# Attention and mixture-of-experts block on one core: half of the first quad's score maxima taken inside the feature loop, and the last chunk's waves and features moved into the first quad

## The reference, cut to what matters

```python
x = _layernorm(x + attention(x))       # x: (2, 2048, 256), f32
x = _layernorm(x + moe_ffn(x))         # 8 experts, the top 2 per token

# attention, 16 heads of 16 dimensions
q, k, v = split(x @ Wq), split(x @ Wk), split(x @ Wv)
q_amp, k_amp = _amp_norm(q), _amp_norm(k)      # softplus, then divided by the root mean square over a head
q_phi = math.pi * jnp.tanh(split(x @ Wqp))
k_phi = math.pi * jnp.tanh(split(x @ Wkp))
scores_phase = (q_amp*cos(q_phi)) . (k_amp*cos(k_phi)) + (q_amp*sin(q_phi)) . (k_amp*sin(k_phi))
scores = (q . k + lam * scores_phase) / 4      # causal
out = softmax(scores) @ v @ Wo
```

## Time and profile before

| what | us |
|---|---|
| runs: median (lowest to highest of 3) | 1952.91 (1946.81 to 1959.45) |
| the profiled execution, its own time | 1948.98 |
| its span, first to last instruction | 1947.3 |
| PE busy, 89% of the span | 1737.1 |
| DVE busy, 65% | 1262.3 |
| ACT busy, 45% | 882.6 |
| POOL busy, 19% | 366.4 |
| mean granted TensorE clock, share of full speed | 0.941 |

### The profile page before, as it was taken

How to read it: one execution, slowest core, us unless ns; L and a number is a source line. 1 busy time by engine, 2 the same in 40 slices (tenths; PEclk the granted TensorE clock), 3 DMA queues, 4 the chain that set the end, 5 groups by cost and what they waited for, 6 DMA issues and landing times.

```text
span 1947.3 us, 28314 instructions
## 1 busy us (share of the span) xinstructions
PE 1737.1 (89%) x9130; PEld 920.4 (47%) x9131; DVE 1262.3 (65%) x2992; ACT 882.6 (45%) x1035; POOL 366.4 (19%) x478
## 2 busy tenths in 40 slices
PE   6998479999999999999999999977639999999965
PEld 3444234444444444444444444426525666666644
DVE  3677867777777777777777777516525555555536
ACT  2677524455555555555455554544311221221236
POOL 0111211111121111211211112103572111111111
PEclk9999768899999999999999999997759999999988
DMA  3366434011021020110201103016521111111144
GB/s 102 137 238 236 179 129 147 7 36 70 8 73 39 15 90 7 57 50 7 99 12 39 67 7 121 13 60 204 205 95 38 47 43 48 44 43 49 44 132 151
DMA packets 99497, 155.30 MB, mean 80 GB/s; under 512 B 10752, under 2 KB 60736, under 8 KB 99008
## 3 DMA queue, kind: packets, MB, share of 16 engines
q1 hardware_dynamic: 84928, 122.53, 18.9%
q0 software_dynamic: 14464, 31.40, 4.6%
HBM read 87.90 MB, written 65.35 MB: 79 GB/s over the span
## 4 chain that ended last, share of the span: by engine, by line
PE 70%; DVE 8%; ACT 7%; issue 6%; DMA 5%; POOL 2%; SPq 1%; another core or an unknown queue 0%; ACTq 0%; DVEq 0%; POOLq 0%
PE att_ps_s L884 22%; PE exp_ps_h L1564 13%; PE att_ps_o L903 12%; PE att_ps_m L862 10%; PE exp_ps_y L1582 6%; ACT att_probs L931 3%; DMA out_parts<-att_out_t 2%; PE pre_ps_q L311 2%; PE exp_ps_t L1572 2%; PE pre_ps_h L311 1%; DVE att_maxima L945 1%; DMA k_parts<-pre_waves 1%; PE exp_ps_x L1553 1%; POOL sorted_rows L1449 1%; DMA route_a_inv<-inv_rows 1%
## 5 line engine op out<-in xcount | busy, mean ns | idle before, releaser
L931 ACT ACTIVATE att_probs<-att_ps_s 128x1024 f32<-128x1024 f32 (+3 forms) x640 | 563.7, 895 | 484.4 <-PE att_ps_s L884 476.5
L884 PE MATMUL att_ps_s<-att_queries,att_keys 49*128 49x512 f32 (+3 forms) x2560 | 632.8, 561 | 20.9 <-ACT att_probs L931 11.4
L945 DVE TENSOR_REDUCE att_maxima<-att_ps_m 128x1 f32<-128x512 f32 x768 | 487.1, 684 | 153.6 <-PE att_ps_m L862 148.6
L862 PE MATMUL att_ps_m<-att_keys,att_queries 48*128 48x512 f32 (+3 forms) x1280 | 506.5, 605 | 24.1 <-DVE att_maxima L948 15.9
L862 PEld LDWEIGHTS att_ps_m<-att_keys,att_queries 48*128 48x128 f32 x1280 | 197.7, 193 | 315.8 <-DVE att_maxima L945 141.4
L884 PEld LDWEIGHTS att_ps_s<-att_queries,att_keys 49*128 49x128 f32 x2560 | 242.9, 191 | 127.3 <-ACT att_probs L931 85.4
L948 DVE CUSTOM_DVE_ANT_0 att_ps_m<-att_ps_m,att_future 128x128 f32<-128x128 f32 (+3 forms) x512 | 240.3, 514 | 73.4 <-PE att_ps_m L862 72.1
L903 PE MATMUL att_ps_o<-att_probs,att_values 128*32 128x512 f32 (+3 forms) x2560 | 269.3, 535 | 11.1 <-POOL att_probs L1034 11.1
L1564 PE MATMUL exp_ps_h<-keep_w,exp_rows_t 128*128 x568 | 257.4, 596 | 5.5 <-DVE exp_rows_t L1598 5.5
L1640 ACT ACTIVATE exp_hidden<-exp_product 128x512 f32<-128x512 f32 x71 | 44.8, 632 | 343.7 <-DVE exp_product L1623 343.7
L1034 POOL TENSOR_SCALAR_AFFINE_SELECT att_probs<-att_probs 128x512 f32<-128x512 f32 x128 | 81.1, 634 | 491.3 <-ACT att_probs L931 491.2
(11 more groups left out here) (179 smaller groups left out, 1458.6 us busy)
## 6 DMA issues: line engine op xcount, KB each, us to landing
att_queries<-q_parts SPq DMA_DIRECT2D x64, 192.0 KB
att_keys<-k_parts SPq DMA_DIRECT2D x64, 192.0 KB
exp_rows<-sorted_rows SPq DMA_DIRECT2D x71, 129.0 KB, 2.3
v_rows<-pre_v_sb SPq DMA_DIRECT2D x8, 1024.0 KB, 7.1
q_parts<-pre_waves SPq DMA_DIRECT2D x16, 512.0 KB, 4.2
k_parts<-pre_waves SPq DMA_DIRECT2D x16, 512.0 KB, 5.8
att_values<-v_rows SPq DMA_DIRECT2D x32, 256.0 KB
out_parts<-att_out_t POOLq DMA_DIRECT2D x32, 256.0 KB, 6.0
```

Of the source, the lines that this page charges most:

```text
L862: pe.matmul(take()[:, 0:width], queries[g % 2][half, c, r, P * q:P * q + P], keys[g % 2][half, k, r, 0:width], start=True, stop=True).then ...
L884: mm = pe.matmul(score_tile(unit, first, last)[:, e], keys[g % 2][half, k // TPC, r, P * (k % TPC):P * (k % TPC) + P].bitcast(F32), querie ...
L931: act.activation(probs[:, step % PROBS, DUO * r:DUO * r + DUO, first:last], score_tile(unit, first, last), ACT.Exp, scale=SCALE).then_inc( ...
L945: dve.tensor_reduce(to, buf[:, 0:width], AX.X, ALU.max).then_inc(s_mr, 1)
```

## The change

1. `Maxima` holds what the maxima need, and is made before `prepare`. In the passes of the feature loop that project chunks 4 to 7, PE puts two products of the maxima behind each half projection (`send_early`, eight times a pass), and DVE has eight `take_early` in its list, which take those two tiles each. Together these are the first 64 of quad 0's 160 tiles: chunks 0 and 1 whole, and a third of chunk 2. They use a ring of two banks: the products of a turn wait until the tiles of the turn before are read.
2. The banks of that ring come from `ps_n`: the norm sum of the queries now goes to `ps_q`, with two waits more (L519 waits for both copies of q, the projection of q for the logarithm of that sum).
3. The square of the amplitudes goes from POOL to ACT, as the second stage of its list, behind the first tanh and ahead of the norm's exponential.
4. On DVE the cosine features (`features`, f = 0) now stand ahead of `keep_qk` of the keys, where they stood behind it.
5. PE's list is unrolled.
6. Chunk 7's cosine and sine (ACT) and its features (DVE) are left out of `prepare`. ACT does them ahead of the exponentials of step 4 of quad 0, DVE at the values of step 3.
7. `Plan` begins with those 64 tiles done, and has the costs of item 6. The ones under the keys of the second buffer are written by SP instead of POOL, behind the last store of the features.

```diff
-            def square(i, p):
-                pool.wait_ge(s_amp, i + 1)
-                if since(i, 1):
-                    pool.wait_ge(s_norm, 2 * i)
-                pool.tensor_tensor(amp_sq[:, :], amp[:, p], amp[:, p], ALU.mult).then_inc(s_sq, 1)
-
-            pipelined(pool, NCH, [(square, 1)])
...
+    def send_early(self, pe):
+
+        for _ in range(DUO):
+            tile, self.sent = self.sent, self.sent + 1
+            if tile >= len(self.ring):
+                pe.wait_ge(self.s_mr, tile - len(self.ring) + 1)
+            self.send(pe, self.ring[tile % len(self.ring)], *self.early[tile])
+
+    def take_early(self, dve):
+
+        if self.taken == 0:
+            dve.wait_ge(self.s_const, 1)
+        for _ in range(DUO):
+            tile, self.taken = self.taken, self.taken + 1
+            self.take(dve, self.ring[tile % len(self.ring)], tile, *self.early[tile])
...
-            def project(weight, out, p):
+            def project(i, weight, out, p, ready):
 
                 for c in range(2):
                     for k in range(DK):
                         mm = pe.matmul(out[:, c], weights[:, weight, k, c * P:(c + 1) * P], x_t[:, p, k],
                                        start=(k == 0), stop=(k == DK - 1))
-                return mm
+                    if c == 1:
+                        mm.then_inc(ready, 1)
+                    if i in EARLY_CHUNKS:
+                        maxima.send_early(pe)
...
+            def square(i, p):
+                act.wait_ge(s_amp, i + 1)
+                if since(i, 1):
+                    act.wait_ge(s_norm, 2 * i)
+                act.activation(amp_sq[:, :], amp[:, p], ACT.Square).then_inc(s_sq, 1)
...
             pipelined(act, NCH, [
                 (lambda i, p: phases(i, p, Q), 1),
+                (square, 2),
                 (lambda i, p: norm_exp(i, p) if i < NCH - 1 else None, 3),
                 (soft_exp, 1),
...
             pipelined(dve, NCH, [
+                (take_early, 1),
                 (lambda i, p: keep_qk(i, p, Q), 1),
+                (take_early, 1),
                 (abs_phase, 2),
+                (take_early, 1),
                 (norm_amplitudes, 3),
+                (take_early, 1),
+                (lambda i, p: features(dve, i, p, 0) if i < NCH - 1 else None, 3),
+                (take_early, 1),
                 (lambda i, p: keep_qk(i, p, K), 1),
-                (lambda i, p: features(i, p, 0), 3),
+                (take_early, 1),
+                (take_early, 1),
+                (take_early, 1),
                 (keep_v, 1),
                 (amplitudes, 1),
                 (keep_x, 0),
-                (lambda i, p: features(i, p, 1), 3)])
+                (lambda i, p: features(dve, i, p, 1) if i < NCH - 1 else None, 3)])
...
             for step in range(QUADS * STEPS):
+                if step == LATE_STEP:
+                    features.last_waves(act)
...
                 elif event == "values":
                     keep_out(*what)
+                    if tuple(what) == (0, LATE_STEP - 1):
+                        features.last_features(dve)
```

More of the change, by code:

```diff
@@ L164, in absolute @@
     return dve.tensor_scalar(out.bitcast(U32), in_.bitcast(U32), 0x7FFFFFFF, None, ALU.bitwise_and)
-def prepare(nc, block, small, x, Wq, Wk, Wv, Wqp, Wkp, lambda_raw, q_parts, k_parts, v_rows, first_quad):
+BLOCKS = [TPC * (c + 1) for c in range(QC)]
+FIRST = [sum(BLOCKS[:c]) for c in range(QC)]
+STEPS = sum(BLOCKS)
+QUADS = B * NQ
+CHUNKS = QUADS * QC
+QUAD_LOADS = 16 * (2 * DUO + 1)
+MAX_TILES = [DUO * DUO * TPC * (c + 1) for c in range(QC)]
+SLOTS_PS = 3
+SLOTS_S = 2
+PROBS = 6
+BATCH = 2
+AHEAD = 3
@@ L172, in prepare @@
+def prepare(nc, block, small, x, Wq, Wk, Wv, Wqp, Wkp, lambda_raw, q_parts, k_parts, v_rows, first_quad, maxima):
     with ExitStack() as stack:
@@ L241, in prepare, with make_waves, features, last_waves @@
         rows_v = v_rows.rearrange("(c t p) w -> c p t w", p=P, t=TPC)
+        def make_waves(act, i, p):
+            act.wait_ge(s_absp, i + 1)
+            act.activation(waves[:, p, 0], waves[:, p, 0], ACT.Sin, bias=half_pi, scale=-PI_BELOW).then_inc(s_wave[0], 1)
+            act.wait_ge(s_tanh, 2 * i + 2)
+            if since(i, 2):
+                act.wait_ge(s_out[2][p], STORED * (i >> 1))
+            act.activation(waves[:, p, 1], phase[:, p], ACT.Sin, scale=PI_BELOW).then_inc(s_wave[1], 1)
+        def features(dve, i, p, f):
+            dve.wait_ge(s_an, i + 1)
+            dve.wait_ge(s_wave[f], i + 1)
+            for c in range(2):
+                dve.scalar_tensor_tensor(waves[:, p, f, c], normed[:, c], lam_scale[:, c:c + 1], waves[:, p, f, c],
+                                         ALU.mult, ALU.mult).then_inc(s_feat, 1)
+            dve.tensor_tensor(waves[:, p, f, 2:4], normed[:, 2:4], waves[:, p, f, 2:4], ALU.mult).then_inc(s_feat, 1)
+        def last_waves(act):
+            make_waves(act, NCH - 1, (NCH - 1) % 2)
+        def last_features(dve):
+            for f in range(2):
+                features(dve, NCH - 1, (NCH - 1) % 2, f)
         @block.sync
@@ L595, in __init__ @@
         self.kept_at, self.negated_at, self.placed_at = {-1: 0}, {}, {}
+        self.group = EARLY_GROUPS
+        self.turns = list(range(self.groups[EARLY_GROUPS][0]))
+        self.negated_at = {n: 0 for n in self.turns}
     def run(self, engine, ns, ready):
@@ L814, in attend, with put_ones @@
         vacated = {"max": s_mr, "turn_max": s_row}
-        CONSTS = 1
-        LOADS = 16 * (2 * DUO + 1)
+        def put_ones(eng, i):
+            eng.wait_ge(s_made, 1)
+            for e in range(DUO):
+                row = HALF * e + FEAT
+                eng.dma_start(keys[i][row:row + 1].rearrange("p c r t -> p (c r t)").bitcast(F32),
+                              ones[0:QC * DUO * CH // (P // 2)]).then_inc(s_one[i], 16)
         def chunk_row(g, c):
@@ L853, in take @@
                 return ps_m[buffer]
-            def max_tile(n, r, q, k, e):
-                g, c = divmod(n, QC)
-                if (r, q, e) == (0, 0, 0):
-                    pe.wait_ge(s_qkv[g % 2][c], LOADS * (g // 2 + 1))
-                width = CH if k < c else P * (q + 1)
-                half = slice(HALF * e, HALF * e + FEAT)
-                pe.matmul(take()[:, 0:width], queries[g % 2][half, c, r, P * q:P * q + P],
-                          keys[g % 2][half, k, r, 0:width], start=True, stop=True).then_inc(s_mt, 1)
             def turn_max(n):
@@ L913, in _ @@
                 elif event == "max":
-                    max_tile(*what)
+                    highest.send(pe, take(), *what)
                 elif event == "turn_max":
@@ L977, in invert @@
                 dve.reciprocal(inverse[:, n % 2], sums[:, n % 2]).then_inc(s_inv, 1)
-            tile = 0
+            tile = DUO * EARLY_GROUPS
             for event, *what in plan:
                 if event == "max":
-                    take_max(*what, tile, ps_m[slots.pop(0)[0]])
+                    highest.take(dve, ps_m[slots.pop(0)[0]], tile, *what)
                     tile += 1
-                    if tile == sum(MAX_TILES[m % QC] for m in range(what[0] + 1)):
-                        negate(what[0], tile)
                 elif event == "turn_max":
@@ L1002, in _ @@
             pool.memset(ones[:, :], 1.0).then_inc(s_made, 1)
[L1003 to L1016 removed]
+            put_ones(pool, 0)
+            made.make(pool)
             def place_max(n):
```

218 lines of the change are left out of this document (110 added, 108 removed).

## The result

The changed kernel takes 1982.46 us (median of 4 runs, 1976.50 to 1986.53) against 1952.75 us before (4 runs, 1946.81 to 1959.45): a ratio of 1.0143, with a 95% interval of 1.0114 to 1.0172. It is slower by 1.4%, within 1.5 us of the forecast. The profiled execution took 1986.53 us, and its span 1984.9.

What follows compares the result with a forecast made beforehand. A pass was taken to be bound by a chain of waits of nearly 24 us through the engines. Loop +49, last pass and drain +15.3, first quad -36.3: +28 us, 1981 us against 1952.91; range 1969 to 1993.

Steps and rivals of the forecast that it cites:

- Passes 2 and 3: Loop passes of chunks 2 and 3: square and cosine features join the chain, 28.3 us each, +8.8 us in all.
- The square: On ACT in each pass, ahead of the norm's exponential that DVE waits for: +1.9 us, no table load.
- The features ahead of the keys' copy: DVE's cosine features in each pass, now on the chain before the copy of the keys' q: +2.5 us.
- Passes 4 to 6: Loop passes of chunks 4 to 6: PE and DVE tied by the two-bank ring, 37.5 us each, +40.6 us.
- one fall of the clock: In each pass with early tiles, PE restarts at 1.2 GHz behind a 5.4 us gap: +1.9 us.
- Chunk 7 and the drain: Last pass with the drain, to chunk 7's normed amplitudes: 58.8 us, not 43.5 (+15.3).
- To step 12: From chunk 7's normed amplitudes to step 12's values in quad 0: 59.5 us, not 95.8 (-36.3).
- The late waves: Chunk 7's waves on ACT in the first quad, with two table loads: 6.5 us, PE idle about 5 us.
- What stood at nothing: SP's quad 1 loads some 30 us later; first maxima come a chunk and a half after step 12: no cost.
- Turns slip into gaps: Rival, early-tile passes: takes wait on nothing, 30.5 us a pass, no change, 1949 us; chance 0.18.
- Work sets the passes: Rival, early-tile passes: PE's work of 26.4 us sets each pass, not latency; faster, 1925 us; chance 0.08.
- The clock stays low: Rival, early-tile passes: PE at 1.2 GHz from the keys' half on, +28 us more, 2009 us; chance 0.10.

Runs made afterwards that it cites:

- norm sum behind v: The changed kernel with PE's norm sum of the queries written behind the value projection instead of ahead of it: 1984.01 us, ratio 1.0165 to before.
- features behind: The changed kernel with DVE's cosine features moved behind the copy of the keys' q: 1994.38 us, ratio 1.0196 to before.
- square behind: The changed kernel with ACT's square behind the norm's exponential instead of ahead of it: 1966.86 us, ratio 1.0063 to before.
- loop order: The changed kernel with ACT's square behind the norm's exponential, DVE's takes four and five ahead of normed amplitudes, cosine features behind take six: 1951.93 us, ratio 0.9995.
- the best order: The loop order kernel with chunk 7's waves and features also back in the feature loop, uncharged in the plan: 1936.89 us, ratio 0.9923 to before.
- takes ahead: The changed kernel with DVE's fourth and fifth take ahead of the normed amplitudes instead of behind them: 1981.98 us, ratio 1.0146 to before.

## Why the prediction was right, step by step

- **Passes 2 and 3, forecast 28.3 each.** Measured 29.2 and 30.6; the term was 3.2 us too small in all. The square was sized right: with the features out of the way it is 25.7 less 23.9 = 1.8 us. The features ahead of the keys' copy were put at 2.5 and cost 3.5 and 4.9, and the traces show what else came: the queries' norm sum now waits for that copy too (it starts at 82.72, the copy ends at 82.62), PE stands 3.9 us, and norm sum and v run at a lower clock (0.76 of full speed from 82.72 to 89.70; v 4.74 us, 3.62 usual), in the second pass for longer (0.63 from 111.93 to 120.20). The prediction had no such wait. That this wait alone is the reason is not shown: with it gone (norm sum behind v) a later one took its place.
- **Passes 4 to 6, forecast 37.5.** Measured 37.5, 36.8 and 37.1, by the mechanism named: the take behind the normed amplitudes, PE idle 5.21 us (5.4), one fall of the clock. It cost 3.47 - 1.98 = 1.5 us here, and 1.8 in the next pass (3.78 at 216.67), for the 1.9 forecast. (Its 3 x 13.5 = 40.6 is 40.8 by 37.5 less 23.9; nothing hangs on it.) But the split inside was wrong in one step: "cosine features 19.2, fifth take 20.4, copy of the keys' q" put the features on the chain, while "features behind" shows that they fill a wait of DVE's there. What the runs give for the 13.2 us over 23.9 is, as means of the three passes: 2.7 for the square (square behind), 1.9 for the order of DVE (loop order against square behind: 3.6, 0.2 and 2.1), and 8.6 for the tiles that remain in the loop order (7.0 to 10.3).
- **Chunk 7 and the drain, forecast 58.8.** 57.8; the normed amplitudes end at 293.71 where 293.4 was given.
- **To step 12, forecast 59.5.** 55.8. The first scores started at 296.48, 2.8 us behind the mark and not 6.1. The copies and the issue came as forecast (293.63 and 294.19), but the DMA of the row was put at the 4.96 us of the kernel before, where loads of features ran beside it; here it took a median of 1.6 us and was over before PE was done with its next tiles. The late waves held PE for 4.00 us (5 forecast), with 1.28 + 2.00 + 1.89 + 1.28 = 6.45 us on ACT.
- **What stood at nothing.** That SP's loads come late was put at nothing, as first used a chunk and a half after step 12. No tile waited for them, but the loads of the next stage's weights, queued behind on SP (357.85 to 380.6), now meet the DMA of chunk 3's row, and that row came 3.2 us later against its turn than before. The term put at nothing was worth these 3.2 us, at a place the prediction did not look at.
- **The rivals.** *Turns slip into gaps* falls. The 30.9 us of the loop order are near its 30.5 by accident: its 30.5 are 28.3 and 2.2 for four turns, and there the pass without tiles is 23.9 and the tiles cost 7.0. *Work sets the passes* falls, even in the best order, where passes stay 4.5 to 6 us above the 26.4 us of PE's work; PE is idle for a fifth of passes 4 to 6 in the changed kernel and for 12% there. *The clock stays low* falls: 0.89 through passes 4 to 6, one fall in each.
- **The clock's share.** Four returns of the clock were read behind 4 to 8 us of idle time: 3.47 us for 1.98 (half projection), 4.74 for 3.62 (v), 6.29 for 3.70 (the projection in "norm sum behind v"), and 3.78 for 1.88 (norm sum, 279.18). The first three lie on the chain, at 1.1 to 2.6 us each. The fourth does not: ACT reads that sum only at 286.05, behind a table load that waits for DVE. By the Trainium skill (TensorE: Matmul & The Clock Gate, "What's actually happening") the ramp penalty is under 1% of a typical kernel's span. The figures here agree: at 1.9 us in each of four passes, the estimate of the prediction, it is 7.6 us or 0.4% of 1984.9. Against a change of 29.7 us that is a quarter.

The sum was +28 and the measurement +29.7. That they are so close is luck in part. The passes of chunks 2 and 3 (3.2) and the row of chunk 3 (3.2) were some 6 us too cheap; the first quad up to step 12 was 3.7 us too dear, passes 4 to 6 together 1.1, and the last pass with the drain 1.0.

What stays open: why the charge costs less (7.5 us) when the late work is there than when it is not (17.7), if it does; one trace of each was read, and the spread of single marks was not measured. That the weights' loads delay the row was read from the traces and not tried by itself: the wait is there in the kernels whose row is issued beside the loads and gone where it is issued behind them, but these kernels differ in more.

## What to carry to other kernels

Where two engines alternate through a ring of one turn, an order of work is one chain through both lists: moving a single item can move the wait (takes ahead, norm sum behind v) or uncover another (features behind). On DVE only the moves together shortened it, by 0.7% or some 13 us. Before work is moved into a later stage, ask what the planner is told about it: the charge reordered TensorE's list, and without the work behind it that order cost 0.77%. An item that nobody needs soon, as the square here, goes behind the one that another engine is waiting for; that single move won 0.8%.

## What was not expected of the hardware

The DMA of a row of maxima, 4.0 KB, took three times as long beside large loads. In the changed kernel the two pieces issued from 387.94 us on, while the loads of the weights (2048.0 KB each) were under way, took a median of 4.7 us from issue to landing; the two issued from 406.87 on, with the loads done, took 1.6. Beside the smaller loads of features (335.94) it was 3.2. The two lines of the DMA view over 330 to 400 us, changed kernel, where the median is of the four pieces at 335.94 and 387.94:

```profile
keep_w<-in_L_ffn_W_dram SPq DMA_DIRECT2D x4, 2048.0 KB, 17.6
...
att_queries<-att_max_row POOLq DMA_DIRECT2D x4, 4.0 KB, 4.6
```

The square in ACT's chain needed no table load between the tanh and the exponential: the three start at 171.38, 172.30 and 174.09 and last 1.02, 1.90 and 1.90 us, with nothing between.
